# The first of eight images laid anew: gram by chunk, correlation ahead of ranks and late weights, ties for all tiles at once, ScalarE shares, and six banks behind the token transposes

## The reference

```python
x = x + L0(gn(x))   # relu(W0 @ [feature; 25 local correlations] + b0)
x = x + L1(gn(x))   # silu(in_proj), depthwise conv of 3 taps + silu, selective scan
                    # over tokens in a permuted order, * silu(gate) + res, silu(out_proj)
x = x + L2(gn(x))   # W2 @ x + b2
x = x + L3(gn(x))   # W3 @ x + b3
```

## Time and profile before

| what | value |
|---|---|
| median of three runs | 1847.55 us (1846.09 to 1850.96) |
| profiled execution | 1856.14 us, its span 1854.3 us |
| PE busy | 1723.8 us, 93% of the span |
| DVE, ACT, POOL busy | 59%, 46%, 22% |
| mean granted PE clock | 0.983 |

### The profile page before, as it was taken

One profiled execution on the slowest core, in us unless ns is written; L12 is line 12 of the kernel. 1 busy time (PEld: TensorE's weight loads), 2 busy tenths in 40 slices (PEclk: granted clock), 3 DMA queues, 4 the chain that ended last, 5 costly groups with the idle time before them and its releaser, 6 DMA issues.

```text
span 1854.3 us, 23766 instructions
## 1 busy us (share of the span) xinstructions
PE 1723.8 (93%) x8573; PEld 951.1 (51%) x8573; DVE 1097.6 (59%) x2186; ACT 860.1 (46%) x1045; POOL 416.3 (22%) x425
## 2 busy tenths in 40 slices
PE   3576999999999999999999999999999999998988
PEld 2242654545545555456545565455554565454643
DVE  6777566544756547546665457565475456751665
ACT  3444544463445542555444644455425553444432
POOL 0403222043110330223210331103302231103220
PEclk9887999999999999999999999999999999999999
DMA  6202221133102331122311331023311233113201
GB/s 223 61 23 90 87 92 26 69 120 125 37 24 80 110 124 38 69 72 91 104 29 69 120 128 35 24 82 108 125 38 58 74 100 105 28 46 97 69 23 46
DMA packets 124634, 142.27 MB, mean 77 GB/s; under 512 B 52307, under 2 KB 101523, under 8 KB 124510
## 3 DMA queue, kind: packets, MB, share of 16 engines
q1 hardware_dynamic: 110462, 105.27, 17.9%
q0 software_dynamic: 12288, 34.68, 5.7%
q10 hardware_dynamic: 1760, 0.71, 0.1%
HBM read 80.62 MB, written 60.01 MB: 76 GB/s over the span
## 4 chain that ended last, share of the span: by engine, by line
PE 64%; DVE 12%; issue 7%; DMA 6%; ACT 4%; POOL 3%; another core or an unknown queue 3%; DVEq 0%; SPq 0%; POOLq 0%; ACTq 0%
PE bank L1467 61%; POOL d_scan L450 2%; DMA rows<-d_scan 2%; DMA rows<-d_norm 1%; DVE bn L850 1%; PE bank L1742 1%; PE bank L1675 1%; DMA d_scan<-rows,rank 1%; DVE gate L1212 1%; DVE gate L1023 1%; DVE res L1146 1%; PE bank L1620 1%; DVE res L1148 1%; DVE x_odd L1121 1%
## 5 line engine op out<-in xcount | busy, mean ns | idle before, releaser
L1467 PE MATMUL bank<-buf_a,win_hi 128*128 128x512 f16 x1536 | 463.2, 384 | 19.7 <-ACT gate L599 11.2
L1467 PE MATMUL bank<-buf_a,win_lo 128*128 128x512 f16 x768 | 294.0, 383 | 0.0
L1467 PE MATMUL bank<-buf_b,w_hi 128*128 128x512 f16 x960 | 287.9, 382 | 4.0 <-DVE buf_b L922 4.0
L1467 PEld LDWEIGHTS bank<-buf_a,win_hi 128*128 128x128 f16 x1536 | 149.7, 99 | 203.9 <-issue 28.4
L1467 PE MATMUL bank<-gate,w_out 128*128 128x512 f32 x512 | 228.9, 594 | 4.2 <-DVE gate L1214 4.2
L450 POOL DMA_INDIRECT d_scan<-rows,rank x128 | 125.2, 978 | 349.4 <-DVE rows L1183 313.5
L1467 PE MATMUL bank<-buf_b,w_lo 128*128 128x512 f16 x480 | 183.2, 382 | 0.0
L1467 PE MATMUL bank<-buf_a,w_hi 128*128 128x512 f16 x576 | 172.7, 381 | 1.8 <-DVE x_odd L1121 1.7
L467 POOL DMA_INDIRECT rows<-d_y,rank x128 | 123.0, 961 | 135.4 <-DMA d_y<-buf_b 89.7
L1467 PEld LDWEIGHTS bank<-buf_b,w_hi 128*128 128x128 f16 x960 | 94.1, 99 | 113.9 <-DVE buf_b L922 4.2
L1467 PEld LDWEIGHTS bank<-gate,w_out 128*128 128x128 f32 x512 | 94.5, 190 | 111.8 <-issue 99.5
(11 more groups left out here) (225 smaller groups left out, 2822.3 us busy)
## 6 DMA issues: line engine op xcount, KB each, us to landing
rows<-d_scan SPq DMA_DIRECT2D x16, 1092.0 KB, 5.7
d_y<-buf_b SPq DMA_DIRECT2D x64, 256.0 KB, 2.1
work<-in_x SPq DMA_DIRECT2D x28, 512.0 KB, 4.4
d_gram<-rows SPq DMA_DIRECT2D x32, 260.0 KB, 2.6
x_even<-in_x SPq DMA_DIRECT2D x16, 512.0 KB
x_odd<-in_x SPq DMA_DIRECT2D x16, 512.0 KB
out_x<-x_even SPq DMA_DIRECT2D x16, 512.0 KB, 2.6
out_x<-x_odd SPq DMA_DIRECT2D x16, 512.0 KB, 2.6
```

Of the source, the lines that this page charges most:

```text
L1467: return eng.matmul(out, lhsT, rhs, start=start, stop=stop, skip_group_check=True, **kw)
```

## The change

All parts but the first touch only image 0 (and what image 0 does for image 1).

- `in_bank`: units 10 to 17 go round six banks (4, 5, 6, 3, 2, 1, ...) instead of two. Units 10 to 13 wait for the tokens' evacuations, later ones for the last unit in the same bank. This holds for all eight images. `factor_rows(0, 0)` waits for the evacuation of unit 17 instead of the tokens'.
- PE's gram of image 0 goes chunk by chunk, each as soon as its split is there; its PSUM is emptied by ACT instead of DVE. The first split stands inside `scales`. L0's low weights follow the splits directly.
- `score_step` 0 to 2 stay at the splits; 3 to 13 are spread over DVE's later work. SP issues the correlation's transfers first, then the score rows and the late weights. DVE does the correlation factors ahead of ranks and maxima; L2's and L3's maxima move to the splits in front of image 0. PE does the second exchange after the fourth `l0_main` unit and starts `l0_corr` after the sixth.
- ACT spreads `in_weights` between the L0 evacuations; POOL's `in_low` and `l0_add` are reordered, the last `in_low` comes last. PE's first in-unit waits for the low weights chunk by chunk.
- Ranks: equal scores are counted once per head for all eight tiles by three instructions; a step is then two. None lies in L0 now; image 0 has 1, 2, 2, 2 and 1 steps for head 0 around the convs and all eight of head 1 behind `row_ready`.
- The conv's first tap of image 0 is done by ACT (`first_tap`).
- `rest_lows` moves behind `scan_masks(m, 0)`.
- Image 0 no longer prepares image 1 early: no `early`, `early_stats`, `variance`, `bias` there. Image 1's statistics are taken by `input_stats` from its loaded x behind the fourth `gated`, PE's `gn_sum(m + 1, 0)` goes behind `out_part(4, 1)`, and normalizations and splits go between the output units.

```diff
-        in_bank = (3, 4, 6, 1, 2, 1, 2, 1) + (2, 1) * 8
+        in_bank = (3, 4, 6, 1, 2, 1, 2, 1, 2, 1, 4, 5, 6, 3, 2, 1, 4, 5) + (2, 1) * 3
...
-                if not last:
+                if not (first or last):
                     wait(eng, "gn_split1", m, KC)
                     early(0)
...
             in_low(0)
+            l0_add(0, 0, 0)
             in_low(1)
-            l0_add(0, 0, 0)
+            l0_add(0, 0, 2)
             in_low(2)
-            l0_add(0, 0, 2)
-            in_low(3)
             l0_add(0, 0, 4)
             l0_add(0, 0, 6)
+            in_low(3)
             rstd(0, 1)
...
+                for t in range(NT):
+                    a, z = (64 if t == 0 else 0), (WIN - 64 if t == NT - 1 else WIN)
+                    wait(eng, "gram_mm", 0, (t | 1) + 1)
+                    act(gram[:, t, 2 + a:2 + z], gram_ps(t)[:, a:z], ACT.Copy).then_inc(s["gram_ev"], 1)
...
+                def first_tap(k):
+                    if first:
+                        wait(eng, "in_evac", m, 2 * k + 2)
+                        if k >= 2:
+                            wait(eng, "tok_mm", m, k - 1)
+                        mid = par[:, TAP + 3 * k + 1:TAP + 3 * k + 2]
+                        act(conv_out[:, k % 2, :], conv_in[:, k, 1:N + 1], ACT.Identity, bias=par[:, BCONV + k:BCONV + k + 1],
+                            scale=mid).then_inc(s["conv_mac"], 1)
...
+                if first:
+                    for u in range(8):
+                        if 3 <= u < 7:
+                            normalize(m + 1, 0, u - 3, X[1 - z])
+                        out_evac(m, u)
...
             in_weights(0)
-            in_weights(1)
             shifts_copy(0, 0)
             shifts_copy(0, 1)
             eng.wait_ge(s["par_in"], 16 * 8)
             l0_evac(0, 0)
             l0_evac(0, 1)
-            in_weights(2)
+            in_weights(1)
             l0_evac(0, 2)
             l0_evac(0, 3)
+            in_weights(2)
+            l0_evac(0, 4)
+            l0_evac(0, 5)
             in_weights(3)
...
+                    TT(cmp_row, row_scores, own.unsqueeze(1).broadcast_to([P, P, NT]), ALU.is_equal).then_inc(s["p_count"], 1)
+                    TT(cmp_row, cmp_row, after.unsqueeze(2).broadcast_to([P, P, NT]), ALU.mult).then_inc(s["p_count"], 1)
+                    eng.tensor_reduce(counts[:, 2, NT * h:NT * h + NT], cmp_row.rearrange("p n t -> p t n"), AX.X, ALU.add).then_inc(s["p_count"], 1)
...
-                STT(cmp_tile[:, 0, :], tile, own, after, ALU.is_equal, ALU.mult).then_inc(s["p_count"], 1)
-                for a, (start, n, op) in enumerate(((0, t, ALU.is_le), (t + 1, NT - 1 - t, ALU.is_lt))):
+                for a, (start, n, op) in enumerate(((0, t, ALU.is_le), (t, NT - t, ALU.is_lt))):
...
-                STT(cmp_tile[:, 1, :], tile, own, cmp_tile[:, 0, :], ALU.is_lt, ALU.add).then_inc(s["p_count"], 1)
-                eng.tensor_reduce(counts[:, 2, q:q + 1], cmp_tile[:, 1, :], AX.X, ALU.add).then_inc(s["p_count"], 1)
...
                 if first:
-                    ranks(7)
-                    rest_lows()
+                    ranks(8)
-                if not last:
+                if not (first or last):
                     early_stats(m + 1, 1)
                     moments(m + 1, 0)
                     variance(m + 1, 0)
                 scan_masks(m, 0)
+                if first:
+                    rest_lows()
+                    eng.wait_ge(s["w_lo_rest"], 2 * KC)
...
                 gated(3, 1, 1)
+                if first:
+                    input_stats(m + 1, 1 - z)
                 gated(4, 2, 0)
                 gated(5, 3, 0)
-                if not last:
+                if first:
+                    variance(m + 1, 0)
+                elif not last:
                     split(m + 1, 0, 0)
                 gated(6, 2, 1)
                 gated(7, 3, 1)
-                if not last:
+                if first:
+                    bias(m + 1, 0)
+                elif not last:
                     split(m + 1, 0, 1)
...
                 for u in range(8):
                     out_unit(m, z, u)
+                    if first and 2 < u < 7:
+                        split(m + 1, 0, u - 3)
...
+                        elif 10 <= q < 14:
+                            wait(eng, "tok_ev", m, 3 if q < 12 else 4)
                         elif q > 4:
-                            wait(eng, "in_evac", m, q - 1)
+                            wait(eng, "in_evac", m, max(p for p in range(q) if in_bank[p] == in_bank[q]) + 1)
...
                 filler(5)
-                if not last:
+                if not (first or last):
                     gn_sum(m + 1, 0)
                 filler(4)
...
                 out_part(4, 1)
+                if first:
+                    gn_sum(m + 1, 0)
                 wait(eng, "y_res", m, 5)
```

More of the change, by code:

```diff
@@ L379, in _ @@
             correlation(0)
+            eng.wait_ge(s["p_score"], SCORES)
+            for h in range(HEADS):
+                eng.dma_start(d_score[h], score_col[:, NT * h:NT * h + NT]).then_inc(s["score_out"], 16)
+            eng.wait_ge(s["score_out"], 16 * HEADS)
+            for h in range(HEADS):
+                eng.dma_start(score_rows[h], d_score[h].rearrange("p q -> (p q)").unsqueeze(0).broadcast_to([P, N])).then_inc(s[f"score_in{h}"], 16)
+            eng.wait_ge(s["w_lo_L0"], KC + 1)
+            weights("L2")
+            weights("L3")
             images(eng, image)
@@ L443, in image @@
                 for h in range(HEADS):
-                    if h and not last:
+                    if h and not (first or last):
                         rstd(m + 1, 0)
@@ L823, in maxima, with scales @@
                     ins.then_inc(s["w_max"], 1)
-            def scales(first, n, rnd):
+            def scales(first, n, rnd, between=None):
                 eng.wait_ge(s["w_maxt"], rnd + 1)
@@ L955, in _, with corr_weight_low @@
             eng.tensor_reduce(par[:, 44:45], wmax[:, 0:5], AX.X, ALU.max).then_inc(s["w_maxc"], 1)
-            scales(0, 1, 0)
-            for k in range(KC):
-                split(0, 0, k)
-                for n in range(4 * k, min(4 * k + 4, 14)):
-                    score_step(n)
-            def low_l0():
-                for n, (k, v) in enumerate(wchunks["L0"]):
-                    eng.wait_ge(s["w_hi_L0"], n + 1)
-                    low("L0", k, v).then_inc(s["w_lo_L0"], 1)
+            scales(0, 1, 0, lambda: split(0, 0, 0))
+            split(0, 0, 1)
+            score_step(0)
+            score_step(1)
+            split(0, 0, 2)
+            score_step(2)
+            split(0, 0, 3)
+            for n, (k, v) in enumerate(wchunks["L0"]):
+                eng.wait_ge(s["w_hi_L0"], n + 1)
+                low("L0", k, v).then_inc(s["w_lo_L0"], 1)
+            def corr_weight_low():
                 eng.wait_ge(s["w_hi_L0"], KC + 3)
@@ L1194, in image @@
                 scan_masks(m, 0)
-                if not first:
+                if first:
+                    rest_lows()
+                    eng.wait_ge(s["w_lo_rest"], 2 * KC)
+                else:
                     eng.wait_ge(s["x_out"], m * per["x_out"])
@@ L1232, in image @@
                     out_unit(m, z, u)
-                    if u == 0:
+                    if first and 2 < u < 7:
+                        split(m + 1, 0, u - 3)
+                    if u == 0 and not first:
                         split(m + 1, 0, 2)
-                    if u == 2:
+                    if u == 2 and not first:
                         split(m + 1, 0, 3)
@@ L1456, in _ @@
             bias(0, 1)
-            for k in range(KC):
-                split(0, 1, k)
-                if k == 0:
-                    ranks(1)
+            maxima("L2", [v for _, v in wchunks["L2"]], 9)
+            split(0, 1, 0)
+            maxima("L3", [v for _, v in wchunks["L3"]][0:2], 13)
+            split(0, 1, 1)
+            maxima("L3", [v for _, v in wchunks["L3"]][2:4], 15)
+            split(0, 1, 2)
+            split(0, 1, 3)
             images(eng, image)
@@ L1855, in _ @@
             l0_main(3)
+            exchange(1, 1)
             l0_main(4)
+            shifts_to_rows(0, 0)
             l0_main(5)
-            shifts_to_rows(0, 0)
             shifts_to_rows(0, 1)
-            for u in range(6):
-                l0_corr(0, u)
+            eng.wait_ge(s["w_lo_L0"], KC + 1)
+            l0_corr(0, 0)
+            l0_corr(0, 1)
             for u in (6, 7):
```

135 lines of the change are left out of this document (68 added, 67 removed).

## The result

| | before | after |
|---|---|---|
| median of 4 runs | 1848.84 us (1846.09 to 1850.96) | 1826.89 us (1825.13 to 1827.88) |
| ratio, 95% interval | | 0.988 (0.9867 to 0.9893) |
| profiled execution | 1856.14 us, span 1854.3 | 1825.13 us, span 1823.3 |
| PE busy in it | 1723.8 us | 1719.2 us, 94% |

What follows compares the result with a forecast made beforehand. Image 0 up to the scan was taken as bound by chains through DVE, ACT, POOL and SP, not PE. 27.6 + 3.5 + 5 = 36 us off the profiled 1856.1 gives 1820; 33 off 1847.55 gives 1814.5; range 1801 to 1831.

Steps and rivals of the forecast that it cites:

- The start: Image 0 up to its first unit: gram 8.4 us earlier, ACT's weights 4.1, first unit at 85.6, a gain of 10.4.
- Conv and tokens: Image 0's convs and ranks: tokens(3) at 126.2 instead of 138.46, 2 us more gained, 12.3 in sum.
- the step has slack: Image 0's convs: ACT's first tap takes longer than DVE's did, but was claimed to cost nothing.
- rival (a): Ranks bind behind head 1's whole-head work; new operations 3.6 instead of 1.22 us each: 1821 to 1825, chance 0.13.
- To the scan: From tokens to first factor_rows: 17.74 us wait goes, factor_rows at 161.1 with a 2.6 us PE wait, gain 31.7.
- Head 1: Head 1's scatter, reload and masks in image 0: reload lands near 168, masks end before PE asks near 170; no loss.
- The end of image 0: Image 1's preparation, now uncovered before its gram, loses 4.1 us; image 0 as a whole gains 27.6.
- Six banks: PE's gate waits removed: 3.5 of 3.9 us in the loop images, 5 of 7.3 in image 7.
- (b): Image 0's uncovered end costs twice as much, or ACT's L0 list grows: 5 to 12 us more, 1820 to 1827, chance 0.10.
- (c): Better than the sum: DVE's L0 addition goes first, low weights don't bind, all ACT waits go: 1801 to 1805, chance 0.09.
- (d): Head 0's scatter and reload start no sooner because row_ready is late, so the stall stays: 1842 to 1848, chance 0.04.
- (e): Slower: POOL's scatters and DVE's whole-head comparisons exclude each other, needing a 34 us slip of ranks(8); chance 0.03.

Runs made afterwards that it cites:

- a_early: Changed kernel with image 1's early preparation put back under the scan, where the kernel before had it; ratio 0.9922 to the kernel before.
- c_ranks: Changed kernel with ranks moved earlier: two steps into the scales' wait, head 1's whole-head comparison ahead of the fourth conv; ratio 0.9898 to the kernel before.
- b_banks: Kernel before with the six banks alone, image 0's order left old; ratio 1.0004 to the kernel before.
- c_early: Changed kernel with image 1 prepared early again, in places DVE has free, and two ranks moved into the scales' wait; ratios 0.9871 and 0.9821 to the kernel before.
- c_both: As c_ranks, with rest_lows also put ahead of head 0's masks; ratio 0.9896 to the kernel before.
- a_tail: Changed kernel with two gated products between the halves of image 1's statistics and PE's sum for image 1 moved back; ratio 0.9898 to the kernel before.

## Why the prediction was right, and where not

The time lies inside the stated range, but not inside the forecast's own 1806 to 1821: the gain is 11 us short of the 33. The stall for the sum went and `factor_rows` moved as worked out; head 1's chain and the six banks did not.

- The start: right. Gram 24.33 (24.7), ACT's weights 49.31 (50.7), first unit 83.25 (85.6), so 12.8 instead of 10.4. The addition held by POOL took 3.49 (3.59 was assumed), at the forecast place.
- Conv and tokens: 127.31 against 126.2, near by luck. From the first unit to `tokens(3)` it took 44.1 us, against 42.4 in the kernel before; 2 us less were forecast, and the start, 2.4 us better than forecast, covered most of that. That "the step has slack" failed: DVE waits 3.40 us for ACT's first tap ahead of the fourth conv, and PE 2.28 at `tokens(1)`. The whole-head comparisons took 1.22 and 1.23; the reduction took 2.02 instead of 1.22, 0.8 us per head, part of rival (a) and small. The Trainium skill ("VectorE: DVE Perf Modes", The perf-mode tier table) gives this reduction one rate for every type and says nothing of order; a maximum over 1536 elements in order took 1.75, so 1.17 for 1024 as an estimate by that rule, and here the permuted f16 read took 2.02. The measurement decides.
- To the scan: right. Scatter 135.09 (133.3), then 11.6 us to the reload's issue (11.6), masks done at 153.47 (152.0), PE's wait 2.59 (2.6), `factor_rows` 162.60 (161.1). 30.2 instead of 31.7.
- Head 1: a failed step that cost 4 us. "I count nothing, with 1 us of slack": from `factor_rows` to the load's issue it took 45.5 us, against 41.4 in the kernel before and 41.2 in a_early, where nothing is late. That is 4 us. The reload landed at 171.6 instead of near 168; "landing after 171" stood among the signs of a wrong prediction. Of these 3.6 us, 2.0 are the scatter's later start (152.29 instead of 150.3) and 1.6 the scatter and the reload themselves (19.3 us instead of 17.7). In c_ranks that stretch takes 41.0 us again, but `factor_rows` comes 3.1 us later, since the two scatters of 10 us each and the two reloads then meet and PE stops among the transposes; so earlier ranks alone win next to nothing.
- The end of image 0: right. 36.0 and 37.8 us from load to gram against 33.1, so 2.9 to 4.7 lost where 4.1 was forecast. The 1.9 us between the two executions are nearly all the slower six products.
- Six banks: the largest failed step. 3.5 us in the loop and 5 in image 7 were forecast, and b_banks gives 0.7 us slower, within -1.8 to +3.5. I had taken the sum of the removed waits for the gain. "The new wait is never later than the old" was true and not enough: what was late next, head 0's reload, stood in the trace of before as the wait of DVE for `rows<-d_scan`, and I asked for it in image 0 but not in the loop.

By terms: 27.6 for image 0 became 23.2 (31.7 - 1.5, 4.1 lost at head 1, 2.9 at the end), and 8.5 became nothing; 23.2 agrees with the 22 of the medians. By the second execution of the changed kernel image 0 won 21.5. The rivals: (a) was near in its place, the chain behind the ranks, but not by the price of the three new operations. (b) has the measured time at the top of its 1820 to 1827, but not its cause, since the end cost what was forecast and the start came earlier than forecast. (c), (d) and (e) are out.

## What to carry to other kernels

A wait that is removed is worth what the next wait on the same engine leaves of it: before pricing it, look in the same stretch at what the other engines wait for, here DVE's 5 us for a reload in every image. Two errors that cancel, as 2.4 us at the start and 3.5 in the convs here, make a place look rightly forecast; compare stretches as well as places. A preparation that leaves a cover should be looked at as a chain with its own fixed length (33 against 36 to 38 us), and it may fit into idle time elsewhere, as in c_early, which has neither the stall nor the longer end. Where runs differ by 5 us, fixed places in the trace say more than medians, but they too moved by 0.2 to 3.1 us between two executions of one kernel here, so a second execution belongs to each.

## What the runs showed of the hardware

The indirect transfers of image 0 took 0.96 us each in most places, and often longer while DVE ran the eight `rest_lows` (two inputs in SBUF) beside them: 1.49, 1.02, 1.02, 1.02 from 153.55 to 158.00 in the changed kernel, and 1.17, 1.02, 1.02, 1.02 from 145.10 to 149.22 in c_both, where `rest_lows` stood at 144.69, with 0.96 right behind in both. But in a_tail the first two beside `rest_lows` took 0.96 (153.32 and 154.58), in c_ranks the one beside it as well (155.02), and in the changed kernel the last took 1.44 at 161.85, 3 us after `rest_lows` had ended, so another cause isn't ruled out. Of head 0's transfers the first, beside a whole-head comparison of the ranks, took 1.21, but 1.19 in the kernel before as well; those from 136.61 on took 0.96. Beside `rest_lows` that sums to under 1 us; by the Trainium skill ("SBUF — State Buffer", Who interferes with whom), as I had used it, these should not meet at all; the page calls that an inference.

TensorE's clock came out differently behind the same waits. In the changed kernel's first execution the six output products behind waits of 0.68 and 0.97 us took 2.84 us (clock 1.00 from 224 to 228); in its second, behind 0.86 and 0.97, they took 4.54 (0.57), as in c_ranks behind 1.34 and 0.97 (0.62). Behind head 1's wait it is the other way round: 3.02 us and a mean clock of 0.89 from 165 to 180 in the first execution, 3.03 us and 1.00 in the second. So whether the clock falls to 1.2 GHz behind a short wait is not settled by that wait's length here, and 1.7 us of one execution hang on it.
